# A four-layer sequence model: three low parts moved ahead of convolutions, row loads moved, another head and two output buffers in the scans

## What is computed

```
xm, z = split(h @ W_in)                      # 1024 channels each
xm = silu(causal_conv(xm, width 4) + conv_b)
dtr, Bm, Cm = split(xm @ W_xp)               # 64, 16, 16
dt = softplus(dtr @ W_dt + b_dt); A = -exp(A_log)
for t: hst = hst * exp(dt_t * A) + (dt_t * x_t) * B_t     # 1024 channels x 16 states
       y_t = sum over states of hst * C_t
y = (y + xm * D) * silu(z)
x = x + gate * (y @ W_out)
```

## Time and profile before

| | |
|---|---|
| median of 3 runs | 6273.09 us (6269.48 to 6273.27) |
| profiled execution, its span | 6283.99 us, 6281.9 us |
| input stages of layers 2 and 3 (first row work to the last low part) | 2234.8 to 2899.2 us, 4253.8 to 4922.7 us |
| scans of layers 2 and 3 | 2904.7 to 4249.5 us, 4928.2 to 6281.9 us |
| mean granted TensorE clock | 0.971 of full speed |

### The profile page before, as it was taken

The page is one execution under the profiler, slowest core; times in us unless marked ns, Lnnn a source line. Parts: engine busy times, 40 slices in busy tenths (PEclk is TensorE's granted clock), DMA queues, the critical chain, the costliest instruction groups (busy, mean ns, idle before and its releaser), DMA issues. The chain is left out here.

```text
span 6281.9 us, 85971 instructions
## 1 busy us (share of the span) xinstructions
PE 5507.6 (88%) x30568; PEld 3521.0 (56%) x30568; DVE 4683.8 (75%) x5712; ACT 4204.6 (67%) x6218; POOL 2479.7 (39%) x1098
## 2 busy tenths in 40 slices
PE   8989999998899989996788888888999678888886
PEld 3446666664455534443666666653444466666664
DVE  3349999996555545555999999984554699999996
ACT  2238888884232235556989898973555699999994
POOL 0000000000000000002999999971000499999997
PEclk9999999999999999997999999998999899999999
DMA  6453343323311033335656566633443655656566
GB/s 235 181 143 78 82 88 82 85 52 132 116 44 51 27 119 148 147 137 178 163 155 163 155 164 155 165 86 108 150 150 136 198 146 156 156 154 160 156 157 209
DMA packets 571257, 842.72 MB, mean 134 GB/s; under 512 B 100672, under 2 KB 240064, under 8 KB 570832
## 3 DMA queue, kind: packets, MB, share of 16 engines
q1 hardware_dynamic: 559312, 811.92, 44.3%
q0 software_dynamic: 5120, 16.78, 0.8%
q10 hardware_dynamic: 6400, 8.52, 0.4%
HBM read 544.23 MB, written 292.81 MB: 133 GB/s over the span
## 5 line engine op out<-in xcount | busy, mean ns | idle before, releaser
L1982 POOL TENSOR_TENSOR scan_hC<-scan_h,scan_Crep 128x1024 f32<-128x1024 f32 x1024 | 2395.4, 2372 | 2396.9 <-DVE scan_h L2235 2363.6
L2161 ACT ACTIVATE scan_a<-scan_dt,scan_A 128x512 f32<-128x512 f32 x2048 | 1368.4, 697 | 89.2 <-DVE scan_h L2235 71.8
L2031 PE MATMUL scan_y<-ident,scan_hC 128*128 128x128 f32 x8192 | 1115.2, 280 | 301.4 <-POOL scan_hC L1982 296.1
L2031 PEld LDWEIGHTS scan_y<-ident,scan_hC 128*128 128x128 f32 x8192 | 906.5, 142 | 687.0 <-POOL scan_hC L1982 638.7
L2235 DVE TENSOR_TENSOR_SCAN scan_h<-scan_a,scan_carry,scan_h 128x512 f32<-128x512 f32 x1024 | 1216.9, 1260 | 22.2 <-ACT scan_a L2161 19.4
L2235 DVE TENSOR_TENSOR_SCAN scan_h<-scan_a,scan_h 128x512 f32<-128x512 f32 x1024 | 1155.7, 1200 | 60.9 <-ACT scan_a L2161 60.3
L2137 ACT COPY scan_h<-scan_drive 128x1024 f32<-128x1024 f32 x1024 | 1041.7, 1017 | 179.9 <-PE scan_drive L2019 166.7
L2019 PE MATMUL scan_drive<-scan_Bd,scan_dT 128*128 128x256 f32 x4096 | 751.7, 306 | 134.8 <-ACT scan_h L2137 78.6
L2019 PEld LDWEIGHTS scan_drive<-scan_Bd,scan_dT 128*128 128x128 f32 x4096 | 559.6, 193 | 187.7 <-issue 101.3
L861 DVE CUSTOM_DVE_ANT_0 att_sm<-att_S,att_mneg 128x1024 f32<-128x1024 f32 x512 | 621.8, 1215 | 16.0 <-POOL att_mneg L787 15.8
L919 ACT ACTIVATE att_pr<-att_sm,att_nmax 128x1024 f32<-128x1024 f32 x512 | 590.5, 1153 | 57.9 <-DVE att_nmax L861 45.0
(11 more groups left out here) (189 smaller groups left out, 6173.9 us busy)
## 6 DMA issues: line engine op xcount, KB each, us to landing
scan_dT<-scratch_dtuT SPq DMA_DIRECT2D x512, 256.0 KB, 6.4
scratch_dtuT<-ssmin_dT SPq DMA_DIRECT2D x128, 512.0 KB, 3.3
scan_Crep<-scratch_bc SPq DMA_DIRECT2D x64, 1024.0 KB, 9.5
att_q<-scratch_q_split SPq DMA_DIRECT2D x256, 128.0 KB, 4.5
att_k<-scratch_k_split SPq DMA_DIRECT2D x256, 128.0 KB, 4.7
scratch_uD<-ssmin_uD SPq DMA_DIRECT2D x64, 512.0 KB, 3.4
scratch_z<-ssmin_zt SPq DMA_DIRECT2D x128, 256.0 KB, 2.3
scratch_dt<-ssmin_dt SPq DMA_DIRECT2D x64, 512.0 KB, 2.6
```

The lines of the kernel that those rows point to most:

```text
L1982: nc.gpsimd.tensor_tensor(hC[k % 2][:], of, Crep[:, 2 * p:2 * p + 2, :], ALU.mult).then_inc(s["scaled"].handle, 1)
L2031: last = nc.tensor.matmul(y[j][:, t, :], hC[k % 2][:, i, t * P:(t + 1) * P], ident[:], start=(p == 0 and i == 0 and t == 0), stop=False, i ...
L2161: nc.scalar.activation(a[(2 * k + i) % 3][:], dt[j][:], ACT.Exp, scale=A[:, m, 2 * p + i:2 * p + i + 1]).then_inc(s["decayed"].handle, 1)
```

## The change

Five edits. None changes what is computed.

1. In both input stages the low parts of block 2 of the batch before are taken ahead of the convolution of block 1 and no longer behind it.
2. In layer 2's input stage the rows of batch it + 2 (it = 0, 1) are loaded at m = 4, ahead of `store_dT(it, 0)`, and no longer at m = 6 behind `store_dT(it, 1)`.
3. At the head of both scans Bd[0] is neither cleared nor loaded by 32 DMAs. One load brings the raw B values of the half (128 x 256) into columns of the tile o, which is free then; DVE adds pieces of the identity to a 128 x 32 diagonal and makes Bd[0] by eight multiplies (`spread`), in the order in which the drives read it; PE's first eight drives each wait for one. DVE clears Bd[1] behind them. SP's and ACT's waits for the clear are gone, and ACT's 16 DMA issues with them; the waits of SP for the clear stand now ahead of the first load into Bd[1].
4. ACT makes the two exponentials of unit 0 ahead of the first four copies.
5. In layer 3 the output tiles alternate between o and x, each with its own semaphore; `gate_o(n)` waits for the store of tile n - 2. Layer 2 keeps one buffer.

```diff
@@ ssm_inputs, sync @@
+                    if gather is None and it + 2 < B and m == 4:
+                        rows.load(sp, it + 2)
                     if it + 1 < B and m in (4, 6):
                         store_dT(it, m // 2 - 2)
-                    if gather is None and it + 2 < B and m == 6:
-                        rows.load(sp, it + 2)
@@ ssm_inputs, vector @@
                 for m in range(IB):
-                    if it and m >= 2:
-                        take_lo(it - 1, m)
+                    if it and m >= 1 and m != 2:
+                        take_lo(it - 1, m if m >= 3 else 2)
                     if it == 0 or m >= 1:
                         convolve(it, m)
@@ scan @@
+        raw, diag, pairs = o[:, 0:NC * NS], o[:, NC * NS:NC * NS + TC], o[:, NC * NS + TC:NC * NS + 3 * TC]
+        SPREAD = 8
+        rows_o = [o] if residual is not None else [o, x]
+        o_out = [core.stage_stored[1], core.stage_stored[7]][:len(rows_o)]
@@ scan, sync @@
+                if half == 1:
+                    w(sp, "cleared", SPREAD + 1)
...
+            sp.dma_start(raw, scr["Bcol"][0, 0].rearrange("j t c e -> (j t) (c e)")).then_inc(raw_in.handle, 16)
             sp.dma_start(A[:], scr["A"][layer - 2].rearrange("i p e -> p i e")).then_inc(s["A_in"].handle, 16)
             load_dt(0)
...
             load_dT(0)
             load_C(0, 0)
-            w(sp, "cleared", 1)
-            load_B(0, range(0, TC, 2))
             for q in range(1, 4):
                 load_C(0, q)
             load_dT(1)
             load_dt(1)
-            w(sp, "cleared", 2)
@@ scan, tensor: make_drive @@
+                if n < SPREAD:
+                    w(pe, "cleared", n + 1)
@@ scan, scalar @@
-            w(act, "cleared", 1)
-            for t in range(1, TC, 2):
-                act.dma_start(Bd[0][t::TC, :, t, :], ...
+            decay(0)
             for n in range(4):
                 lay(n)
             for k in range(LOOP):
-                if k < UNITS_ALL:
+                if 1 <= k < UNITS_ALL:
                     decay(k)
@@ scan, vector @@
-                if n >= 1:
-                    dve.wait_ge(o_out.handle, o_out.at(16 * n))
+                if n >= len(o_out):
+                    stores = o_out[n % len(o_out)]
+                    dve.wait_ge(stores.handle, stores.at(16 * (n // len(o_out))))
...
-            for k in range(2):
-                zeros = zero_eps[:, 1:2].broadcast_to([P, NC * TC * NS])
-                nc.vector.tensor_copy(Bd[k][:].rearrange("p c t n -> p (c t n)").bitcast(F32R), zeros
-                                      ).then_inc(s["cleared"].handle, 1)
+            def spread(n):
+                tt, first = n % 4, n // 4 * GS
+                values = raw.rearrange("p (a o n) -> p a o n", o=1, n=NS)[:, tt::4, :, first:first + GS]
+                places = diag.rearrange("p (o t q) -> p o t q", o=1, q=1)
+                shape = [P, NC // 4, TC, GS]
+                nc.vector.tensor_tensor(Bd[0][:, tt::4, :, first:first + GS].bitcast(F32R), values.broadcast_to(shape),
+                                        places.broadcast_to(shape), ALU.mult).then_inc(s["cleared"].handle, 1)
...
+            dve.wait_ge(raw_in.handle, raw_in.at(16))
+            for n in range(SPREAD):
+                spread(n)
+            zeros = zero_eps[:, 1:2].broadcast_to([P, NC * TC * NS])
+            nc.vector.tensor_copy(Bd[1][:].rearrange("p c t n -> p (c t n)").bitcast(F32R), zeros
+                                  ).then_inc(s["cleared"].handle, 1)
```

39 lines of the change are left out of this document (26 added, 13 removed).

## The result

The changed kernel takes **6231.76 us** (median of 4 runs, 6226.19 to 6235.79) against 6273.18 us for the kernel before (4 runs, 6269.48 to 6276.72). The ratio is 0.9931, with a 95% interval of 0.9919 to 0.9944: 41.4 us less. Predicted were 6231.7 us and a range of 6221 to 6248. The interval of the ratio stands for 35 to 51 us less, so that the two figures agree to a tenth of a microsecond is luck. The profiled execution of after has a span of 6233.9 us, 48.0 less than that of before; what these additional 6.6 us are is told further down.

What follows compares the result with a forecast made beforehand. PE was taken to bound the input stages, a chain the scan heads and DVE the rest of the scans; 18.6 + 18.6 + 4.2 = 41.4 us off the median of 6273.1 gave 6231.7 us, range 6221 to 6248.

Steps and rivals of the forecast that it cites:

- The low parts and the rows: Input stages of layers 2 and 3: earlier low parts and rows shorten PE's waits; 18.6 us gained, between 15 and 20.
- Rival (e): Input stages: ACT's chain behind the later convolution holds block 3 for 2 us a batch; 29 us gained, 6244; chance 0.08.
- The heads: Start of both scans: an earlier first recurrence shortens the scan; 11.1 + 10.5 - 3.0 = 18.6 us gained, ends 10 and 25.
- The first drive: Scan heads: PE's first drive waits for dT and comes 9.5 us after the start, ends 5.8 and 13.2; before 18.98.
- a late dT of block 1: Scan heads: block 1's dT lands late for drive 8, costing 1.5 us a head, ends 0 and 4.
- What comes back at the start of the recurrences: Scan heads: the second exponential stands behind the fifth copy, so an estimated 0.4 us of the gain comes back.
- the early exponential: Scan heads: 2.0 us of table load and exponential move beside the loads; 1.6 us a head gained.
- The multiplies: Scan heads: eight on DVE at 1.23 us each, 9.7 us; DVE free 16.7 us after the start, covered by the chain.
- Rival (c): Scan heads: the multiplies run slow and DVE is last; 6237 at 1.8 us each, 6246 at 2.37; chance 0.12.
- rival (d): Scan heads: multiplies so slow that the kernel gets slower, from 5.1 us each; 6299 at 6 us each; chance 0.02.
- Rival (b): Scan heads: later loads bind, dT of block 0 lands with Crep, block 1's 4 us late; 32 us gained, 6241; chance 0.15.
- The two buffers: End of layer 3: late output tiles wait less for stores, POOL's last gather starts earlier; 4.2 us gained, 0 to 7.

Runs made afterwards that it cites:

- lo_only: Kernel before with only the low parts of block 2 taken ahead of the convolution of block 1; ratio 0.9983, 10.7 us less.
- rows_only: Kernel before with only layer 2's row load moved earlier, to m = 4; ratio 0.9978, 13.8 us less.
- head_only: Kernel before with only the raw load, the eight multiplies and the early exponential at both scan heads; ratio 0.9964, 22.6 us less.
- after_again: The changed kernel once more without an edit, as yardstick on the same chip; ratio 0.9935 to before, 6233.03 us.
- exp_late: Changed kernel with ACT's first exponentials put back behind the four copies; ratio 0.9941 to before, 6233.08 us.
- hold: Changed kernel with the last three Crep loads and block 1's dT and dt held on SP until PE's first drive; 0.9949 to before, 6238.03 us.
- spread_twice: Changed kernel with each of the eight multiplies made twice, PE waiting for the second; ratio 0.9955 to before, 6241.54 us.
- tail_29: Changed kernel with tile 29 gated ahead of the sums of batch 1 on DVE; ratio 0.9932 to before, 6232.48 us.
- bufs_only: Kernel before with only the two output buffers in layer 3; ratio 0.9996, not to be told from no change.
- dT_first: Changed kernel with block 0's dT issued ahead of the raw B values, A and dt; ratio 0.9943 to before, 6239.40 us.

## Why the prediction was right, and where it was not

**The low parts and the rows, 18.6 us: 19.0 measured by the distances, right step by step.** The sum agrees within the 1.6 us a batch by which executions of the kernel before differ. The wait moved to block 4 and fell to 0.86 us (forecast 0.9), the statistics follow without a wait, the last batches lost theirs. The two causes of the one wait were separated by lo_only and rows_only: with one cause gone, 3.60 or 2.19 us of wait stay. Rival (e) is refuted: ACT's chain was to be ready 1.4 us ahead of the low part of block 3, and it is. In layer 3 of after ACT ends the high part of block 3 at 4439.43, and DVE takes the low part at 4440.87, behind its statistics; in layer 2 the two are 2435.10 and 2436.55.

**The heads, 18.6 us: 18.6 measured, but with three small errors that cancel, which is luck.** The first drive was forecast 9.5 us after the start. In seven executions with the raw load first and dT behind dt it came between 9.1 and 10.9 us: 9.6 and 9.1 (head_only), 10.6 and 10.1 (after), 9.6 twice (after_again), 10.2 and 9.3 (exp_late), 10.0 and 9.6 (hold), 10.9 and 9.9 (spread_twice), 9.6 and 10.6 (tail_29), in the mean 9.9. The midpoint between two rows at 5.3 and 12.7 us was thus a good choice, 0.4 us low in the mean and 1.1 and 0.6 low in the profile of after. Against that, the 1.5 us a head for a late dT of block 1 were too much: drive 8 had no wait in after, and even when its loads were held until the first drive it waited only 0.31 us. The landing of 13.8 us with three MB ahead was stretched to four MB and more at the old pace, a pace at which 32 small loads had stood in between; that their absence made the difference is likely, but no run has them and the new order together. What comes back at the start of the recurrences (0.71 and 0.22 us of wait, 0.9) was put at 0.4, and from the first drive to the ninth recurrence after takes 19.85 us and before 20.85, so the early exponential gave 1.0 us a head there and not 1.6. Together: the first drives came 8.4 and 8.2 us earlier than before and not 9.5 and 8.9, the exponentials gave 1.2 too little, and block 1's dT cost 3.0 less than forecast. 3.0 stands against 3.0.

**The multiplies:** 1.15 us each against 1.23 assumed; DVE was free 15.7 us after the start (forecast 16.7). Rival (c) is refuted by the row, and spread_twice shows where its point of decision lies: with 10 us more of multiplies a head loses 5. Here the trace had the last word over the reading of the rule in the Trainium skill that gave rival (c) its first size (Vector Engine (DVE) Microarchitecture Reference, "Measured stream behaviour on trn2"): the source that repeats one word eight times before it moves on doesn't count as one that jumps every element. The same section gives 1.0417 ns for a column and about 75 ns for an instruction, an estimated 1.14 us for 1024 elements, and the trace agrees with that (1.15). So rival (d), which needed over 5 us each, is also off by a factor of more than four.

**Rival (b), loads behind the head that bind,** is refuted by hold: without those 3 MB the first drive comes no earlier. The loads of after's head landed in the order of issue: the raw values 2.1 us after the start, dt by 5.0, when ACT starts on it, dT by 10.6, the first quarter of Crep by 13.0. The price of this rival was added up wrongly: with block 1's dT 4 us late a head would give 11.1 - 3.7 - 4 = 3.4 or 2.8 us, not 4.9 or 4.3, and the time would be 6244 and not 6241. That the DMA engines are full at the head is not quite so in the kernel before (a mean share of 0.81 to 0.89 in the first 13 us, 0.22 in the next 6) but is in after (1.01 to 1.05 from 2.8 to 20.8 us behind the start), and dT is late by what stands ahead of it all the same.

**The two buffers, 4.2 us: 2.7 to 3.3 in the profile of after, the one step whose mechanism failed.** The working let the sums of batch 1 end where they ended before, 32.5 us after the zero point. bufs_only shows that the rest of the working was exact, with tiles 29 to 31 within 0.3 us of it. In after, however, the rows for the sums landed late: DVE waited 7.04 us for them and the sums began 30.8 us after the zero point (29.9 in after_again, 30.6 in tail_29, but 27.8 in bufs_only and 28.0 before), so tile 29 came at 35.3. The eight gathers of batch 1 are issued at the same places in all five (the last of them between 21.6 and 22.0 us), and the 16 DMA engines are over 90% busy in that stretch. What differs is what goes out beside them: ACT's store of batch 0's sums, twice 1 MB, and SP's store of tile 28. ACT's in after and then in bufs_only:

```profile
6186.29 1.00 ACTq L2207 DMA_DIRECT2D out<-scan_h  x2
```
```profile
6219.16 0.99 ACTq L2205 DMA_DIRECT2D out<-scan_h  x2
```

From the zero point ACT's store goes out at 21.3 us in after, ahead of the last gather of batch 1, and at 22.2 in bufs_only, behind it; SP's goes out at 23.8 and 25.4. All eight executions that hold the whole change, or a variant of it, have 21.3 and 23.8, and their sums of batch 1 begin between 29.9 and 31.0. Before, bufs_only and head_only have 22.2 or later and 25.4 or later, and begin between 27.8 and 28.1; in rows_only and lo_only both stores are later still (23.1 and 27.2 for ACT's), and the sums begin directly behind tile 28, at 26.4 and 30.5. So the late landing goes with stores that leave earlier. The working let tile 28 come 0.8 us earlier (it came 1.6) and left the sums of batch 1 where they were; a price for stores that share the busy DMA engines stood only in the lower bound. That the stores are the cause is not shown, since no run moved them alone, and why ACT and PE are 0.9 us further in these executions is open.

**The additional 6.6 us of the profiled pair** are neither of these. DVE's two groups of recurrences, before and then after (busy, mean ns | idle before):

```profile
L2235 DVE TENSOR_TENSOR_SCAN scan_h<-scan_a,scan_carry,scan_h 128x512 f32<-128x512 f32 x1024 | 1216.9, 1260 | 22.2 <-ACT scan_a L2161 19.4
L2235 DVE TENSOR_TENSOR_SCAN scan_h<-scan_a,scan_h 128x512 f32<-128x512 f32 x1024 | 1155.7, 1200 | 60.9 <-ACT scan_a L2161 60.3 <-issue 0.2
```
```profile
L2244 DVE TENSOR_TENSOR_SCAN scan_h<-scan_a,scan_carry,scan_h 128x512 f32<-128x512 f32 x1024 | 1216.6, 1258 | 21.0 <-ACT scan_a L2168 18.2
L2244 DVE TENSOR_TENSOR_SCAN scan_h<-scan_a,scan_h 128x512 f32<-128x512 f32 x1024 | 1155.5, 1198 | 22.8 <-ACT scan_a L2168 13.8 <-ACT scan_h L2148 8.2 <-issue 0.2
```

Of the idle time before, 83.1 us, the heads are 42.9 (21.60, 20.64 and twice 0.33); of that after, 43.8 us, they are 10.0. So 40.2 and 33.8 us stand in the middle of the scans, at single waits of 1 to 3 us whose places differ from one execution to the next. The difference, 6.4 us, with 19.0, 18.6 and 3.3 gives 47.3 of the 48.0. after_again, with no edit at all, has 42.4 us of idle time in place of 43.8, of which 34.0 in the middle. That the 6.4 us are scatter and not an effect of the change is seen in the kernels whose scans were left as they were but for the output buffers: 25.6 us in lo_only, 27.2 in bufs_only, 39.4 in rows_only. The forecast took its terms off the median and not off the profiled execution; that was right, since the medians differ by 41.4 and the three terms measured are 19.0 + 18.6 + 3.3 = 40.9.

## What to carry to other kernels

When one wait has two causes in a row, work out where each moves the next wait: alone, either edit here passed it on (3.60 or 2.19 us left), together they removed 13.5 us in two batches. At a head where nothing but loads and a chain run, list what each engine is ready at (here DVE 15.7, the chain 20.1 us after the start), since a change pays only up to the second of them; after that, reordering the same loads can trade one late operand for another, as dT_first did. When a buffer lets a store leave earlier, ask which loads it now stands ahead of. A term that two far rows bound can be taken from the middle if both ends are kept for the range, and a term below the scatter of the runs is to be read from the profile, at a point shortly in front of it.
